# Feed-forward part eight half states sooner in each chunk, and one butterfly stage of six weight groups on Pool

## The reference

```python
proj = hidden_states @ W_in + b_in              # 512 -> 2 x 1024
hidden, gate = jnp.split(proj, 2, axis=-1)
conv_out = silu(causal_conv4(hidden))
dt_in, Bm, Cm = split(conv_out @ W_x)           # 128, 16, 16
delta = softplus(dt_in @ W_dt + b_dt)
h = exp(delta * A) * h + (delta * x) * B        # per token, 16 states
y = (einsum('bdn,bn->bd', h, C) + conv_out * d) * silu(gate)
return y @ W_out + b_out

x = fwht(x * SU_ug) / SCALE                     # 512 wide
x = silu(x @ W_gate.T * s) * (x @ W_up.T * s)   # 512 -> 2048
x = fwht(x * SU_dp) / SCALE                     # 2048 wide
return x @ W_down.T * (Wscale_dp * SCALE)       # 2048 -> 512
```

## Time and profile before

| | |
|---|---|
| median of 3 runs | 2649.15 us (2647.63 to 2650.23) |
| profiled execution | 2648.38 us, of which the span of the trace is 2646.6 us |
| busy over the span | PE 97%, PEld 82%, DVE 85%, ACT 69%, POOL 77% |
| mean granted clock of TensorE | 0.997 |
| start of chunk 0, 1, 2 (`turn_x`) | 69.47, 217.97, 361.91 us |
| length of chunks 3 to 13 | 151.0 us each |
| chunk 14, chunk 15 | up to 2323.5 us, up to 2470 us |
| tail | from 2470 us to the end |

### The profile page before, as it was taken

One profiled execution on the slowest core, in us unless ns is written; L12 is line 12 of the kernel. 1 busy time (PEld: TensorE's weight loads), 2 busy tenths in 40 slices (PEclk: granted clock), 3 DMA queues, 4 the chain that ended last, 5 costly groups with the idle time before them and its releaser, 6 DMA issues.

```text
span 2646.6 us, 46296 instructions
## 1 busy us (share of the span) xinstructions
PE 2571.5 (97%) x16048; PEld 2183.3 (82%) x16048; DVE 2241.4 (85%) x2573; ACT 1817.6 (69%) x3935; POOL 2046.4 (77%) x1691
## 2 busy tenths in 40 slices
PE   7999989999999999999999999999999999989998
PEld 5566568989888888988888898988888898978888
DVE  6897998899888888898889889898889889889522
ACT  4776777677777777777777767777777777755322
POOL 7776879788787979888797978888797988877222
PEclk9999999999999999999999999999999999999999
DMA  5664246656666665656666665666666666656665
GB/s 181 208 210 167 100 165 217 225 199 240 211 232 219 215 220 207 240 204 233 219 222 221 216 230 192 242 209 237 216 216 220 208 229 207 232 180 226 264 268 185
DMA packets 165209, 564.41 MB, mean 213 GB/s; under 512 B 17264, under 2 KB 19696, under 8 KB 132976
## 3 DMA queue, kind: packets, MB, share of 16 engines
q1 hardware_dynamic: 164976, 561.44, 61.1%
HBM read 527.30 MB, written 34.08 MB: 212 GB/s over the span
## 4 chain that ended last, share of the span: by engine, by line
PE 77%; DVE 11%; ACT 7%; issue 3%; DMA 1%; POOL 1%; SPq 0%; DVEq 0%; ACTq 0%; POOLq 0%
PE pF L726 21%; PE hT L633 14%; PE pM L651 13%; PE pD L742 10%; PE pM L703 8%; DVE h L1180 5%; DVE acc L1193 3%; PE pM L673 3%; PE pD L766 2%; ACT decay L986 2%; PE decay L726 2%; PE hT L625 1%; PE pF L766 1%; ACT delta L963 1%; ACT delta L958 1%
## 5 line engine op out<-in xcount | busy, mean ns | idle before, releaser
L1180 DVE TENSOR_TENSOR_SCAN h<-decay,dbx 128x512 f32<-128x512 f32 x1024 | 1201.1, 1206 | 93.9 <-ACT decay L986 65.2
L1362 POOL TENSOR_TENSOR dbx<-u,bb 128x2048 f32<-128x2048 f32 (+1 forms) x272 | 1179.8, 4338 | 37.8 <-DVE h L1180 35.9
L986 ACT ACTIVATE decay<-delta,a_neg 128x255 f32<-128x255 f32 x2048 | 876.0, 468 | 313.7 <-DVE h L1180 306.4
L1193 DVE SCALAR_TENSOR_TENSOR acc<-hT,bcT,acc 128x1024 f32<-128x1024 f32 x480 | 609.9, 1271 | 120.6 <-PE hT L633 116.8
L726 PE MATMUL pF<-fxT_hi,wug 128*128 128x256 f32 x3632 | 709.9, 288 | 0.7 <-issue 0.7
L633 PEld LDWEIGHTS hT<-ident,h 128*128 128x128 f32 x4096 | 471.6, 141 | 142.0 <-issue 89.6
L726 PEld LDWEIGHTS pF<-fxT_hi,wug 128*128 128x128 f32 x3632 | 582.9, 192 | 1.1 <-issue 1.1
L633 PE MATMUL hT<-ident,h 128*128 128x128 f32 x4096 | 534.3, 273 | 33.2 <-DVE acc L1193 21.4
L726 PE MATMUL pF<-fxT_lo,wug 128*128 128x256 f32 x1816 | 514.3, 283 | 0.0
L651 PE MATMUL pM<-xnT,w_in 128*128 128x256 f32 x2016 | 478.7, 381 | 4.6 <-ACT hid L906 3.2
L651 PEld LDWEIGHTS pM<-xnT,w_in 128*128 128x128 f32 x2016 | 366.5, 191 | 51.8 <-issue 5.0
(11 more groups left out here) (173 smaller groups left out, 2719.7 us busy)
## 6 DMA issues: line engine op xcount, KB each, us to landing
wug<-scratch_ug SPq DMA_DIRECT2D x243, 1024.0 KB, 4.8
wd<-scratch_wd SPq DMA_DIRECT2D x243, 512.0 KB, 3.9
w_in<-in_W_in SPq DMA_DIRECT2D x252, 256.0 KB, 2.9
bb<-scratch_bc SPq DMA_DIRECT2D x128, 256.0 KB, 4.9
xb<-in_hidden_states SPq DMA_DIRECT2D x16, 512.0 KB, 5.2
xr<-in_hidden_states SPq DMA_DIRECT2D x16, 512.0 KB, 5.8
out<-xr SPq DMA_DIRECT2D x15, 512.0 KB, 3.7
kept_ug<-scratch_ug SPq DMA_DIRECT2D x7, 1024.0 KB, 7.6
```

Source lines behind the costliest of these rows:

```text
L986: e = act.activation(da[q % 2][:, i, 1:], delta[c % 2][:, dt, 1:], ACT.Exp, scale=a_neg[:, dt, n:n + 1])
L1180: dve.tensor_tensor_scan(row(h[n % 2][:, tiles, :]), row(da[q % 2][:, :, :]), row(dbx[n % 2][:, tiles, :]), 0.0, ALU.mult, ALU.add).then_i ...
L1193: dve.scalar_tensor_tensor(acc[c % 2][:, tb, :], hT[:, :], cn, acc[c % 2][:, tb, :], ALU.mult, ALU.add).then_inc(acc_done, 1)
L1362: pool.tensor_tensor(dbx[n % 2][:, tiles, :], u[:, tiles, :], rows, ALU.mult).then_inc(done if restarts(c) else prod_done, 1)
```

## The change

(1) All steps of the FF are placed by one function, `feed`, eight half states (`LEAD`) sooner than before; the distances between them stay. `turn_f` moves from k = 1 to k = 25 (`F_SLOT`) of the chunk before, where PE's order is: `turn_f`, `down`, one `dt_proj`, `turn_h`. At k = 26 PE starts with `turn_h`. (2) The steps that make the FF's input move up: `normalise("o")` to k = 18, `moments("o")` to state 9, `add_out` to state 10, `f_stats` to k = 22, `moments("f")` to state 11, `normalise("f")` to k = 23, the load of the residual to k = 14. (3) The FF's last steps move too: `down_evac` to k = 30, `z_stats` to k = 31, `moments("z")` to state 1, `normalise("z")` to k = 4, `add_z` to state 5, the store to k = 10. (4) For six of the eight up and gate groups (`SUMMED`) Pool first makes sums and differences of two halves of the loaded weights (`half_sums`), so that each of their outputs takes two steps on PE and not four; the groups' order, buffers and dealing out change with that, and the transform ends at k = 16 of chunk 1 and not at k = 29. (5) The kept tiles are 4, 6, ... 14 and not 2, 4, ... 12.

```diff
-    KEPT = (2, 4, 6, 8, 10, 12)
+    KEPT = (4, 6, 8, 10, 12, 14)
+        LEAD = 8
+        F_SLOT = SLOTS - LEAD + 1
+        def feed(c, k):
+            steps = ((chunk(c - 1), k + LEAD - SLOTS), (chunk(c - 2), k + LEAD), (chunk(c - 3), k + LEAD + SLOTS))
+            return [(j, p) for j, p in steps if j is not None and p >= -1]
...
-            if ff is not None:
-                T_SEQ += [("f", ff, 0)]
...
-                T_SEQ += [("h", cur, i) for i in range(1, TB * (NST - 1))]
+                T_SEQ += [("h", cur, i) for i in range(1, F_SLOT - 2)]
+            if back is not None:
+                T_SEQ += [("f", back, 0)]
+            if cur is not None:
+                T_SEQ += [("h", cur, i) for i in range(F_SLOT - 2, TB * (NST - 1))]
...
+        UG_LOAD, WD_LOAD, UG_STEP, TANH_STEP, HIGH_STEP, LOW_STEP, DOWN_STEP = (
+            {first + 2 * ft: ft for ft in range(HT)} for first in (-1, 4, 2, 3, 5, 6, 7))
+        F_TURNED, Z_EVAC, Z_STATS, Z_MOMENTS, Z_NORM, Z_ADD = 1, 38, 39, 42, 44, 50
...
+        WHOLE, SUMMED = UG_GROUPS[:2], UG_GROUPS[2:]
-        steps_of = lambda o: 2 if GROUPS[o // KT][0] == "down" else KT
+        steps_of = lambda o: KT if o // KT in WHOLE else 2
+        FIRST_SUM = 18
-                room = (4 if k == 0 or 8 <= k < 16 else 3 if 23 <= k < 28 else 2) if c == 0 else 2
+                at = SLOTS * c + k
+                room = (4 if k == 0 else 3 if k >= 8 else 2) if at < FIRST_SUM else (2, 2, 2, 1, 1)[(at - FIRST_SUM) % 5]
...
                 if k == 0:
                     if front is not None:
                         turn_x(front)
-                    if fold is not None:
-                        down(fold, HT - 3)
+                    for tile in ups:
+                        up_gate(*tile, (1,))
                     if back is not None:
                         turn_h(back, NST - 1, 0)
-                    if fold is not None:
-                        up_gate(fold, HT - 1)
+                    for tile in ups:
+                        up_gate(*tile, (0,))
                     return
                 if k == 1:
-                    if ff is not None:
-                        turn_f(ff)
...
+                if k == F_SLOT:
+                    if back is not None:
+                        turn_f(back)
+                    for tile in downs:
+                        down(*tile)
+                    if front is not None and k in PE_DT:
+                        dt_proj(front, PE_DT[k])
+                    if cur is not None:
+                        turn_h(cur, n - 1, tb)
+                    return
...
+                for j, p in feed(c, k):
+                    if p in HIGH_STEP:
+                        high(j, HIGH_STEP[p])
+                    if p == F_TURNED:
+                        f_hi(j)
...
-                if k == 20 and back is not None:
+                if k == 18 and back is not None:
                     normalise("o", ob, ob, back, on_done)
...
-                if k == 31 and back is not None:
+                if k == 23 and back is not None:
                     normalise("f", ob, xr[back % 2], back, fn_done)
...
-                if k == 29 and back is not None:
+                if k == 22 and back is not None:
                     f_stats(back)
...
+            def half_sums(g):
+                src, dst = had_in[IN_BUF[g]], had_in[SUM_BUF[g]]
+                pool.wait_ge(had_loaded[IN_BUF[g]], 16 * (in_use(g) + 1))
+                if SUMMED.index(g):
+                    pool.wait_ge(had_halved, 2 * SUMMED.index(g))
+                pool.tensor_tensor(dst[:, 0:2, :], src[:, 0:2, :], src[:, 2:4, :], ALU.add).then_inc(had_halved, 1)
+                pool.tensor_tensor(dst[:, 2:4, :], src[:, 0:2, :], src[:, 2:4, :], ALU.subtract).then_inc(had_halved, 1)
...
                 if back is not None:
+                    if n == 9:
+                        moments("o", back)
                     if n == 10:
-                        moments("o", back)
-                    if n == 12:
                         add_out(back)
-                    if n == 15:
+                    if n == 11:
                         moments("f", back)
+                for g in HAD_ADD.get((c, k), ()):
+                    half_sums(g)
```

More of the change, by code:

```diff
@@ L548, in slot @@
                     load_out()
-                if k == 18 and fold is not None:
-                    store_out(fold)
-                if k == 20 and back is not None:
+                for j, p in feed(c, k):
+                    if p == Z_ADD:
+                        store_out(j)
+                if k == 14 and back is not None:
                     load_res(back)
[L553 to L562, removed]
+                for j, p in feed(c, k):
+                    if p in UG_LOAD:
+                        load_ug(j, UG_LOAD[p])
+                    if p in WD_LOAD:
+                        load_wd(j, WD_LOAD[p])
             run(front0, slot)
@@ L707, in _, with up_gate, begin_up_gate @@
             PASSES = ((0, 0), (0, 1), (1, 0))
-            def up_gate(j, ft):
+            def up_gate(j, ft, parts=(1, 0)):
                 no = j * HT + ft
+                if 1 in parts:
+                    begin_up_gate(j, ft, no)
+                for which in parts:
+                    for kt in range(KT):
+                        for i, (a, b) in enumerate(PASSES):
+                            mm = pe.matmul(gate_up_bank(no)[:, which, :], ug_tile(no)[:, 2 * which + a, kt, :], fxT[b][:, kt, :],
+                                           start=(kt == 0 and i == 0), stop=(kt == KT - 1 and i == len(PASSES) - 1))
+                if 0 in parts:
+                    mm.then_inc(ug_mm, 1)
+            def begin_up_gate(j, ft, no):
                 if kept(no) is None:
@@ L722, in up_gate @@
                     pe.wait_ge(scan_done, NQ * NST * NCH)
-                for which in (1, 0):
-                    for kt in range(KT):
-                        for i, (a, b) in enumerate(PASSES):
-                            mm = pe.matmul(gate_up_bank(no)[:, which, :], ug_tile(no)[:, 2 * which + a, kt, :], fxT[b][:, kt, :],
-                                           start=(kt == 0 and i == 0), stop=(kt == KT - 1 and i == len(PASSES) - 1))
-                mm.then_inc(ug_mm, 1)
             def down(j, ft):
@@ L805, in in_slot @@
                         turn_y(back, k - 2)
-                    if ff is not None and k == 2:
-                        up_gate(ff, 0)
+                    for tile in ups:
+                        up_gate(*tile)
                     if front is not None and k == 3:
@@ L820, in in_slot @@
                     hadamard(c, k)
-                if ff is not None and k in UG_SLOT:
-                    up_gate(ff, UG_SLOT[k])
+                for tile in ups:
+                    up_gate(*tile)
                 if front is not None and k in PE_HID:
@@ L830, in in_slot @@
                     x_proj(front, PE_XPROJ.get(k, ()))
-                if ff is not None and k in DOWN_SLOT:
-                    down(ff, DOWN_SLOT[k])
-                if fold is not None and k in DOWN_LATE:
-                    down(fold, DOWN_LATE[k])
+                for tile in downs:
+                    down(*tile)
                 if front is not None:
@@ L1073, in slot @@
                     normalise("x", xb, xb, c + 2, xn_done)
-                if k == 31 and back is not None:
+                if k == 23 and back is not None:
                     normalise("f", ob, xr[back % 2], back, fn_done)
-                if k >= 3 and k % 2 and ff is not None:
-                    tanh(ff, (k - 3) // 2)
+                for j, p in feed(c, k):
+                    if p in TANH_STEP:
+                        tanh(j, TANH_STEP[p])
                 if front is not None and k in ACT_DT and k % 2:
```

114 lines of the change are left out of this document (51 added, 63 removed).

## The result

The changed kernel takes **2687.84 us** (median of 4 runs, 2686.68 to 2688.94), the kernel before 2649.49 us beside it: ratio 1.0144, 95% interval 1.0131 to 1.0157, so 38 us slower. The forecast was 2685 us. The total is right; its parts are so only in the full chunks. In three of the experiments single executions took far longer (4305 to 6639 us), and the ratios leave them out.

What follows compares the result with a forecast made beforehand. PE bounds a full chunk, busy 150.17 of 151.00 us. On 2648.4 us: chunks 0 and 1 0, chunk 2 +5.9, chunks 3 to 13 +44, chunk 14 +3.6, tail -17.4; together +36, 2685 us, range 2646 to 2712.

Steps and rivals of the forecast that it cites:

- Half state 25: In chunks 2 to 14, PE idles 3.0 us per chunk, waiting 1.3 us for delta and 1.5 us for acc.
- Half states 18 to 24: In a full chunk, earlier normalisation of o, add_z and f_stats together cost PE 1.1 us (0 to 2).
- The terms for `add_z` (0.4) and `f_stats` (0.3): Pool's add_z at state 5 may add 0.4 us; DVE's f_stats at k = 22 costs 0.3 us at k = 24.
- The full chunk: 4.8 us of PE idle time (3.0 + 1.1 + 0.7), so 155.0 us, 4.0 more than before.
- Chunk 1: Added FF work, Pool's sums and the new order at its end make this chunk 5 us longer.
- The sums' price: Each of twelve 128x1024 Pool instructions for the transform takes 2.39 us, 14.3 us in each of chunks 0 and 1.
- some 3: In chunk 1, DVE's scan waits some 3 us for the product of state 1, behind the sums of half state 0.
- needs 117 us: PE's work in chunk 1, after transform matmuls leave and 11 us of FF work comes in; DVE needs 131.
- The tail: Four FF tiles leave the end of the kernel, each 2.88 us for gate and up and 1.47 for down: 17.4 us less.
- The idle time: Rival: added idle time at half state 25 is absorbed, chunks stay at 151.0 us, 2632 us in all; chance 0.14.
- The clock: Rival: gaps at half state 25 also lower PE's clock, 13 x 1.9 = 25 us, 2710 us; chance 0.17.
- bound neither by its loads nor by dear sums: Rival: the tail is bound by its loads, or Pool's sums cost the dear price; 15 to 20 us, 2702; chance 0.06.

Runs made afterwards that it cites:

- The first two experiments: Changed kernel, at half state 25: ACT evacuates delta pair 0 before copying turn_f's result, 2666.07 us; separately, PE issues turn_h before dt_proj, 2663.73 us.
- the delta first: Changed kernel, but at half state 25 ACT evacuates delta pair 0 before it copies turn_f's result; 2666.07 us, ratio 1.0057.
- The edits at half states 19 and 25: Changed kernel, separately: o normalised in 19 behind the decays, 2671.64 us; at 25 delta evacuated before the copies, 2666.07 us, or turn_h before dt_proj, 2663.73 us.
- the half tile: Changed kernel with the first FF tile's gate half between turn_h of half states 25 and 26, delta ahead of copies, o normalised at 19; 2669.19 us.

## Why the prediction was right, and where it was not

**Half state 25.** Forecast 3.0 us idle in two waits, of 1.3 and 1.5 us and a little between; measured 1.17 and 1.47, in these places and for these reasons. The first two experiments took each away and the chunk fell by it. `turn_f` to `turn_h` of half state 26 took 7.08 us; I had 7.05.

**Half states 18 to 24.** Forecast 1.1 us; measured 0.58 in the wait and 0.85 by removing its cause. The wait for the decays came out at 4.20 us, as forecast. The terms for `add_z` (0.4) and `f_stats` (0.3) have no row of their own; they were too high or did not exist.

**The full chunk.** 154.7 to 154.8 against 155.0 us: 3.8 and not 4.0 us more, 41.8 of the forecast 44 us in chunks 3 to 13. This carried the result, and all that it needed were rows of single steps of the old trace put into the new order.

**Chunk 1** is the step that failed: forecast 5 us more, measured 15.8; chunks 0 and 1 together 14 us more where the sum had 0. Counted from `turn_x` to DVE's first scan of a half state, the chunk is 9.2 us behind the kernel before at half state 9 (262.59 and 269.85 us in the two traces), 8.3 at 24, 14.3 at 28 (344.51 and 356.85), and 15.8 at its end. (Chunk 0 was forecast 5 us shorter and was 1.9 us shorter; no run settles what took the other 3 us.)

The first loss, up to half state 9, is the transform's: with the transform alone it is 8.9 us, and with the sums all but taken away 2.3. The sums' price (2.36 against 2.39 us) was right, but their wait was 5.1 us and not "some 3", and the waits for the stores were no term at all. With the transform alone the chunk then makes up for most of it and is only 3.6 us behind at half state 28; in the changed kernel, which has tiles of the FF there, it does not.

The second loss, 6 us in half states 24 to 28, falls together with the new order of half state 25 and a lower clock. Here I had it wrong that PE "needs 117 us": PE was busy for 128.24. I had taken matmuls from it at full clock and assumed that the rest would run at full clock too. PE's granted clock was 0.91 in this chunk against 0.99 before, and 0.93 in the kernel with the transform alone. What this costs can be read beside the kernel that normalises o in half state 19, in the stretch from `turn_h` of half state 25 to `dt_proj` behind the FF tile of half state 26. At a granted clock of 0.61 the changed kernel

```profile
344.20 1.63 PE L639 MATMUL hT<-ident,h 128*128 128x128 f32 x8
...
352.92 1.03 PE L696 MATMUL pM<-dtin,w_dt 128*128 128x256 f32 x4
```

takes 8.72 us for it, and at a clock of 1.00 the other

```profile
342.42 1.04 PE L639 MATMUL hT<-ident,h 128*128 128x128 f32 x8
...
348.70 1.03 PE L696 MATMUL pM<-dtin,w_dt 128*128 128x256 f32 x4
```

6.28 us, with the same instructions in the same order, the same wait of 1.47 us between them and the same 1.90 us for the delta ahead of them. So the difference of 2.4 us is the clock's. The rest of this kernel's 4.4 us in chunk 1 (2.1 us) is gained by half state 24, where its edit stands. With the delta first, chunk 1 is 3.35 us shorter, of which 2.4 us are again the same steps at the faster pace and 0.9 us the shorter wait ahead of them. The edits at half states 19 and 25 each took 3.3 to 4.4 us from chunk 1, and two of them together only 4.7: in part they regain the same stretch. What stays open is how the rest of the chunk's loss divides between the added FF work, the stores and the clock.

**The tail.** Forecast 17.4 us less, measured 23.3. The four tiles are right (132 matmuls fewer by the trace: 97 of gate and up, 27 of `down` and one `turn_f` of 8; four tiles are 96 and 24). I had left out that `turn_f` (0.9 us) and the old waits of the tail for products, loads, `fxT_lo` and acc (1.4 + 0.9 + 0.6 + 1.5 us), which are gone: 17.4 + 0.9 + 4.4 = 22.7. With chunk 15, 7 us of gain that I did not see and 2 us too many in the full chunks stand against 14 us of loss in chunks 0 and 1. So the total, 36 forecast and 40.5 measured in the span, is closer than its parts, and that closeness is luck; the time of the full chunks, which sets most of it, is not.

**The rivals.** The idle time was not absorbed: PEld is busy for 131.65 us of 154.68, 85%, and still each microsecond of PE's waits was one of the chunk's. The Trainium skill (Perfetto Trace Analysis, Identifying the Most-Contended Engine) takes the share of the peak rate that is reached and the loads' busy share, and not the matmuls', as the measures of how near a kernel is to roofline. Read as slack that absorbs a new wait, as this rival read it, it fails in this trace; how near the kernel is to roofline is another question, which no run here asks. The clock did not fall in the full chunks (PEclk 1.00), where that rival had put it, but it did in chunk 1, where I had not looked. The tail was bound neither by its loads nor by dear sums.

**Why 41 us less matmul work bought nothing:** in the chain that ended last, PE holds 70 us of chunk 1's 144 before, but only 19 of 150 with the transform alone, where DVE holds 64, ACT 28, Pool 14 and the stores 10. Pool's work grew by 4.7 us for each summed group. And against the gain in the tail (23 us) stand 13 times 3.8 us, since in the old place in_proj filled the turn of hT around `turn_f`, and in the new one nothing did.

## What to carry to other kernels

When a serial piece (turn, copy, subtract, turn) is moved in a loop whose bound engine is full, lay its steps out in microseconds from the old trace in the new order, with the queue of each engine that it passes, and multiply the gaps by the number of turns; a gain at the loop's end is small against them. Before filling a gap with work, see which bank and which queue that work needs itself: the half tile cost 2.25 us until the product that frees its bank was moved too. And where work is taken off TensorE in a stretch that other engines bound, do not price what is left at full clock.

## What the runs showed of the hardware beyond what was expected

The granted clock fell in a stretch where PE kept working: it was 0.68 and 0.57 in windows of 8 us in which PE was busy for 6.06 and 6.53 us, after one with 3.13 us. PE's longest pauses in the 18 us ahead of these windows were of 3.96 us (up to 320.71) and 2.82 us (up to 332.52). In chunk 1 of the kernel with the transform alone, 27.5 us of matmuls less gave 17.6 us less busy time. A store of four outputs of the transform took 6.3 us from its issue in SP's queue,

```profile
255.84 0.38 SPq L496 DMA_DIRECT2D scratch_ug<-had_r_hi  x1
```

to the start (262.18) of the ACT instruction that waited 5.19 us for it, both in the changed kernel. With the stores ahead of the loads, the same store took 4.3 us (253.66 to 257.92).
